# Counting edges into a dense matrix on one core: one register load for two chunks, one count of groups for all tiles, rings of four, and sums copied three windows late

## What is computed

```python
edge_index = jnp.stack([src, dst])
x = _layernorm(x + _L0_gnn_ref(x, edge_index, L0_gnn_gamma), axis=-1)
x = _layernorm(x + _L1_gnn_ref(x, L1_gnn_qW, L1_gnn_kW, L1_gnn_vW, src, dst), axis=-1)
x = _layernorm(x + _L2_gnn_ref(x, L2_gnn_weights, L2_gnn_loop_w, L2_gnn_bias, src, dst, edge_type_8), axis=-1)
x = _layernorm(x + _L3_gnn_ref(x, L3_gnn_W0, L3_gnn_b0, L3_gnn_W1, L3_gnn_b1, L3_gnn_W2, L3_gnn_b2, src, dst), axis=-1)
```

```python
def prop(h):
    return jax.ops.segment_sum(h[src] * norm, dst, num_segments=n)
```

## Time and profile before

| | |
|---|---|
| median of 3 runs | 2363.64 us |
| lowest and highest | 2362.68 and 2366.68 us |
| the profiled execution's own time | 2366.91 us |
| its span, first to last instruction | 2365.2 us |
| busy, share of the span | PE 91%, PEld 76%, DVE 77%, ACT 49%, POOL 37% |
| mean granted clock of TensorE | 0.96 of full speed |

### The profile page before, as it was taken

One profiled execution on the slowest core, in us unless ns is written; L12 is line 12 of the kernel. 1 busy time (PEld: TensorE's weight loads), 2 busy tenths in 40 slices (PEclk: granted clock), 3 DMA queues, 4 the chain that ended last, 5 costly groups with the idle time before them and its releaser, 6 DMA issues. The chain is left out here.

```text
span 2365.2 us, 63175 instructions
## 1 busy us (share of the span) xinstructions
PE 2159.4 (91%) x22505; PEld 1795.4 (76%) x22506; DVE 1832.0 (77%) x2687; ACT 1162.6 (49%) x2789; POOL 879.4 (37%) x1062
## 2 busy tenths in 40 slices
PE   2888888799999999888999978999999999999897
PEld 2777777799999999622222225999996799999787
DVE  8899988765655566578999976988886788887446
ACT  1888888432332333388999966231322432230323
POOL 3444444000000000067888832555552455555000
PEclk8999999899999999989999979999998999999899
DMA  2344444200100000242222224223224322222800
GB/s 67 153 166 165 164 166 159 106 30 30 43 30 30 29 29 15 65 108 57 57 57 59 57 97 159 84 73 88 75 60 127 139 74 77 85 75 45 343 11 22
DMA packets 94785, 205.64 MB, mean 87 GB/s; under 512 B 21718, under 2 KB 61270, under 8 KB 94450
## 3 DMA queue, kind: packets, MB, share of 16 engines
q1 hardware_dynamic: 81458, 182.46, 22.3%
q0 software_dynamic: 13120, 20.18, 4.3%
HBM read 116.99 MB, written 84.76 MB: 85 GB/s over the span
## 5 line engine op out<-in xcount | busy, mean ns | idle before, releaser
L1873 PE MATMUL l_bank<-tab,mask 128*128 128x192 f16 x7600 | 636.3, 247 | 8.3 <-PEq L1704 3.5
L1873 PEld LDWEIGHTS l_bank<-tab,mask 128*128 128x128 f16 x7600 | 629.5, 98 | 10.8 <-issue 10.2
L1459 DVE TENSOR_SCALAR mask<-code 128x1600 int32<-128x1600 int32 x304 | 546.7, 1816 | 91.6 <-PE l_bank L1873 82.7
L1849 POOL DMA_INDIRECT ggot<-table_dram,gidx x408 | 386.2, 947 | 264.7 <-PE l_bank L1873 204.0
L1356 DVE TENSOR_TENSOR pr<-ex,count_copy 128x1568 f32<-128x1568 f32 x200 | 351.0, 1786 | 24.7 <-POOL ex L1255 12.8
L1346 ACT ACTIVATE ex<-score_pair,poss 128x784 f32<-128x784 f32 x400 | 344.0, 910 | 30.0 <-PE score_pair L1294 18.6
L1255 POOL TENSOR_SCALAR ex<-ex 128x1568 f32<-128x1568 f32 x200 | 298.5, 1493 | 78.2 <-ACT ex L1346 71.1
L891 PE MATMUL sums<-onehots,ct 128*128 128x192 f16 x3125 | 266.5, 250 | 11.6 <-issue 7.3
L891 PEld LDWEIGHTS sums<-onehots,ct 128*128 128x128 f16 x3125 | 263.9, 99 | 14.1 <-issue 7.9
L891 PE MATMUL sums<-u,ct 128*128 128x192 f16 x3125 | 259.1, 246 | 0.0
L891 PEld LDWEIGHTS sums<-u,ct 128*128 128x128 f16 x3125 | 258.0, 98 | 0.0
(11 more groups left out here) (344 smaller groups left out, 2873.0 us busy)
## 6 DMA issues: line engine op xcount, KB each, us to landing
code<-code_dram SPq DMA_DIRECT2D x38, 800.0 KB
code_dram<-flat SPq DMA_DIRECT2D x100, 200.0 KB, 1.9
ct_dram<-ct SPq DMA_DIRECT2D x25, 800.0 KB, 3.5
c_dram<-flat SPq DMA_DIRECT2D x25, 800.0 KB, 3.4
ct_again<-ct_dram SPq DMA_DIRECT2D x25, 800.0 KB, 17.3
cring<-c_dram SPq DMA_DIRECT2D x200, 98.0 KB, 1.9
table_dram<-tab SPq DMA_DIRECT2D x50, 384.0 KB, 2.3
flat<-code_dram SPq DMA_DIRECT2D x19, 800.0 KB, 4.4
```

The costliest lines, as they stand in the source:

```text
L1459: e.tensor_scalar(turned.rearrange("p (s q d) -> p s q d", q=NQ, d=DQ // 2), words.rearrange("p (q s d) -> p s q d", q=NQ, d=DQ // 2), abs ...
L1849: e.indirect_dma_start(ggot[:, k, j, :], None, table_dram[:, :], bass.IndirectOffsetOnAxis(ap=gidx[:, k, j:j + 1], axis=0)).then_inc(s_ggo ...
L1873: mm = e.matmul(acc[k][:, 0:2 * D], mask[:, r % MR, s, :], tab[:, s, r, :], start=(r == 0 and s == 0), stop=(r == R - 1 and s == NT - 1))
```

## The change

The counts stage and the last step of its table change:

- The two first chunks of a window are packed into one table entry, the second one times 2048 (FIRST_BITS is 11) plus the first. GpSimd loads one register for a group and takes it apart by a mask and a shift; each chunk number is then limited to 2 NCHP, and `edges` has six more empty columns there.
- One instruction of VectorE takes the maximum of the 25 numbers of groups. Each engine loads it once, before its loop over tiles, and every window runs that many groups.
- `sel` and `col` get rings of four (SELS) instead of two; `col` moves into another buffer.
- ScalarE copies the sums of window w-3 (OUT_LAG) behind the selection of window w. The PSUM ring stays three.
- The first turn round stands after window 2 instead of 1, and its copy `row_out` one window later.

```diff
-                    e.tensor_copy(mi[:, 0:WPS], mc[:, 0:WPS]).then_inc(s_tab, 1)
+                    both_halves = mc[:, 0:WPS].rearrange("t (w h) -> t w h", h=2)
+                    e.scalar_tensor_tensor(mi[:, 0:WPT], both_halves[:, :, 1], float(1 << FIRST_BITS), both_halves[:, :, 0],
+                                           ALU.mult, ALU.add).then_inc(s_tab, 1)
...
-        turned_after = {1: 0, 3: 1, 4: 2, 5: 3}
+        turned_after = {2: 0, 3: 1, 4: 2, 5: 3}
         RECS = 4
+        SELS = 4
+        OUT_LAG = 3
...
-            def groups_of(e, t):
-                return load(e, tile_tab[0:1, bass.ds(t, 1), WPS], 1, NCHP // GRP)
+            def most_groups(e):
+                e.wait_ge(s_top, 1)
+                return load(e, top_groups[0:1, 0:1], 1, NCHP // GRP)
...
                         with e.Fori(0, groups) as g:
+                            e.reg_mov(pair, load(e, tile_tab[0:1, bass.ds(t, 1), w], 0, (1 << 2 * FIRST_BITS) - 1))
                             chunks = []
-                            for h in range(2):
-                                first = load(e, tile_tab[0:1, bass.ds(t, 1), 2 * w + h], 0, 2 * NCHP - GRP)
+                            for by, op in (((1 << FIRST_BITS) - 1, ALU.bitwise_and), (FIRST_BITS, ALU.logical_shift_right)):
+                                e.reg_alu(first, pair, by, op)
+                                e.reg_mov(first, g * GRP + e.snap(first))
+                                e.reg_alu(first, first, 2 * NCHP, ALU.min)
                                 chunks.append(nc.s_assert_within(
-                                    e.snap(g * GRP + first), 0, 2 * NCHP - GRP,
+                                    e.snap(first), 0, 2 * NCHP,
...
                 def _(e):
                     c = Chain(e, s_prep)
+                    e.tensor_reduce(top_groups[:], tile_tab[:, :, WPT], AX_X, ALU.max).then_inc(s_top, 1)
...
-                    n, past, free = three(e, "act")
+                    n = e.alloc_register("cnt_act_done")
+                    past = [e.alloc_register(f"cnt_act_past{k}") for k in range(SELS)]
...
-                        e.reg_mov(free, past)
-                        e.reg_mov(past, n)
+                        free = past[0]
+                        for k in range(SELS - 1):
+                            e.reg_mov(past[k], past[k + 1])
+                        e.reg_mov(past[SELS - 1], n)
...
                     def tile(t, first, second, last=False):
-                        groups = groups_of(e, t)
                         for w in range(WPT):
                             chosen(t, w, groups)
-                            if w >= 2:
-                                window_out(t, w - 2, first)
+                            if w >= OUT_LAG:
+                                window_out(t, w - OUT_LAG, first)
                             elif not first:
-                                window_out(t - 1, WPT - 2 + w, second)
+                                window_out(t - 1, WPT - OUT_LAG + w, second)
```

More of the change, by code:

```diff
@@ L59 @@
 NCHG = -(-NCH // GG) * GG
+FIRST_BITS = 11
 EXP_LOW = math.exp(-10.0)
@@ L390, in gnn_kernel @@
             rec_sv = wqk[:, 114:114 + RECS * 2 * PAIR].bitcast(F16).rearrange("p (k g c) -> p k g c", k=RECS, c=4)
-            sel = wqk[:, 162:162 + 2 * PAIR].bitcast(F16).rearrange("p (k c g) -> p k c g", k=2, c=2)
-            col = wqk[:, 174:174 + PAIR].bitcast(BF16).rearrange("p (k g) -> p k g", k=2)
-            assert 114 + RECS * 2 * PAIR <= 162
+            sel = wqk[:, 162:162 + SELS * PAIR].bitcast(F16).rearrange("p (k c g) -> p k c g", k=SELS, c=2)
+            col_at = 2 * PAIR * (P + WC) + 2 * NW
+            col = onehots[:, col_at:col_at + SELS * PAIR].bitcast(BF16).rearrange("p (k g) -> p k g", k=SELS)
+            assert col_at + SELS * PAIR <= NT * 2 * D
+            assert 114 + RECS * 2 * PAIR <= 162 and 162 + SELS * PAIR <= 2 * D
             s_rec = sem("cnt_rec")
@@ L428, in _, with records @@
                         e.reg_mov(r, 0)
-                    def records(t, w, groups):
+                    groups = most_groups(e)
+                    pair, first = (e.alloc_register("cnt_" + k) for k in ("pair", "first"))
+                    def records(t, w):
                         free = past[0]
@@ L436, in records @@
                         with e.Fori(0, groups) as g:
+                            e.reg_mov(pair, load(e, tile_tab[0:1, bass.ds(t, 1), w], 0, (1 << 2 * FIRST_BITS) - 1))
                             chunks = []
-                            for h in range(2):
-                                first = load(e, tile_tab[0:1, bass.ds(t, 1), 2 * w + h], 0, 2 * NCHP - GRP)
+                            for by, op in (((1 << FIRST_BITS) - 1, ALU.bitwise_and), (FIRST_BITS, ALU.logical_shift_right)):
+                                e.reg_alu(first, pair, by, op)
+                                e.reg_mov(first, g * GRP + e.snap(first))
+                                e.reg_alu(first, first, 2 * NCHP, ALU.min)
                                 chunks.append(nc.s_assert_within(
-                                    e.snap(g * GRP + first), 0, 2 * NCHP - GRP,
-                                    skip_runtime_bounds_check_because="the table's first chunk leaves room for all groups"))
+                                    e.snap(first), 0, 2 * NCHP,
+                                    skip_runtime_bounds_check_because="the minimum is the first of the empty chunks behind the table"))
                             e.wait_ge(s_col, e.snap(free) + 1)
@@ L450, in _ @@
                     with e.Fori(0, NT) as t:
-                        groups = groups_of(e, t)
                         for w in range(WPT):
-                            records(t, w, groups)
+                            records(t, w)
                 @block.vector
@@ L655, in _ @@
                     tile(NT - 1, False, False, True)
-                    window_out(NT - 1, WPT - 2, False)
-                    window_out(NT - 1, WPT - 1, False)
+                    for w in range(WPT - OUT_LAG, WPT):
+                        window_out(NT - 1, w, False)
                     for q in range(NR):
```

29 lines of the change are left out of this document (17 added, 12 removed).

## The result

| | before | changed |
|---|---|---|
| median | 2363.16 us (4 runs) | 2349.6 us (4 runs) |
| lowest to highest | 2361.87 to 2366.68 us | 2345.39 to 2352.06 us |
| the profiled execution's own time | 2366.91 us | 2352.06 us |
| first to last L474 (now L492) | 375.2 us | 360.3 us |
| ratio of the runs, 95% interval | | 0.9935 [0.9919, 0.9951] |

The kernel is 0.65% faster, 15.4 us by the ratio (times 2363.16). I had forecast 35. The sign was right and the time lies at the upper edge of the range, but the gain is less than half of the one forecast. All of it is in the counts stage: 14.9 us by the two traces.

What follows compares the result with a forecast made beforehand. GpSimd's sequencer was taken to bound the counts stage at 14.91 us a tile; at 13.5 us, 24.875 tiles make 335.8, plus 4.3 and 0.3: 340.4 against 375.2, 35 us less. Forecast 2329 us, range 2314 to 2350.

Steps and rivals of the forecast that it cites:

- What bounds the kernel now: Counts stage: GpSimd's sequencer bounds it, 13.46 us of steps plus 1.45 of stretched loads, 14.91 us a tile.
- One load for two chunks: GpSimd's window: one load and two register instructions go, arithmetic comes; 1.59 us falls to 1.41.
- my upper bound: GpSimd's window at worst: fused instructions at 0.141 us each, 0.05 more in L445's own, 1.58 us.
- the whole walk of VectorE: One tile followed at 1.64 us a window on VectorE: 13.1 us plus 0.45 of stalls, 13.5 us.
- One count of groups: GpSimd's step across a tile's end: one load with its pause goes, 0.31 us of the extra 0.74.
- The long loads: GpSimd's loads stretched behind stores: at most all 1.45 us a tile kept, though half as many can be caught.
- What is late next: After GpSimd, VectorE sets the tile: 1.64 us a window, 13.1 us; TensorE 12.4, ScalarE 12.0.
- the two stalls: VectorE waits 0.25 us at window 7 for ScalarE's selection and 0.2 at window 2 for TensorE.
- A: Rival: GpSimd stays the bound through register arithmetic or slowed copies, 14.5 us a tile, 2349 us; chance 0.12.
- D: Rival: lag of three meets ring of three if GpSimd's window stays 1.59 us; 0.6 a tile, 2379; chance 0.04.
- B: Rival: VectorE without stalls, tile 13.1 us, 10 us more gain than forecast, 2319 us; chance 0.2.
- C: Rival: ScalarE's register moves cost 0.05 us a window, tile 13.9 us, 10 us less gain, 2339; chance 0.2.

Runs made afterwards that it cites:

- e4: Changed kernel with fixed chunk numbers instead of GpSimd's table load and arithmetic (counts of the wrong edges): 2336.26 us, ratio 0.9869, stage 346.3 us.
- e7: Changed kernel with each 800 KB store issued as four, packets of 1600 bytes instead of 6400: 2339.99 us, ratio 0.9898, stage 348.9 us.
- e9: Changed kernel with the registers of past counts used in rotation instead of moved along, on GpSimd and ScalarE: 2336.81 us, ratio 0.9882.
- e8: e4 with the sums copied with a lag of two instead of three: 2330.88 us, ratio 0.9859, stage 342.0 us.
- e3: Kernel before with the order alone (rings of four, lag of three, turn rounds after windows 2 to 5), loads as before: ratio 1.0023, 5 us slower.
- e2: Kernel before with one load for two chunks alone, each tile loading its own count: ratio 0.9934, 16 us faster, stage 360.7 us.
- e12: Changed kernel with the sums copied with a lag of two instead of three, nothing else: 2348.55 us, ratio 0.9941, stage 357.6 us.
- e1: Kernel before with the one count of groups alone, loaded once by each engine: ratio 0.9983, 4 us faster, stage 372.3 us.
- e5: Kernel before with one count of groups and both chunk numbers loaded by one instruction into two registers, no arithmetic: 2344.54 us, ratio 0.9927.

## Why the prediction was wrong where it was

*What bounds the kernel now:* right. GpSimd's sequencer set the stage, and the loads held by stores were part of its beat. e4, e7 and e9 each shorten that beat in another way, and the stage follows down to the next bound.

*One load for two chunks:* **this step failed.** I priced the two fused register instructions at 0.08 us each for three operations and took 1.41 us for the window; they take 0.203 and 0.136. With them comes a move of 0.034, the `reg_mov` of `pair` in the diff, which the rows of the order leave out, so that it was four instructions for three. The arithmetic costs 0.034 + 0.032 + 0.203 + 0.136 = 0.405 us and one more pause of some 0.03, where 0.376 went. The two fused instructions at the copies, which were to be dearer at worst, became cheaper, 0.096 to 0.051 us each in the mean, and the window is 1.585 us. That my upper bound was 1.58 is luck: both of its terms were off, and they cancel. What I took from between the bounds was a guess, and the rest of the sum hung on it: with GpSimd at 1.585 us a window it stays the bound, and the whole walk of VectorE, which gave the 13.5 us a tile, does not apply.

*One count of groups:* 0.41 us at a tile's end against 0.31 forecast, 24 times, 9.9 us. This is most of what the change gained.

*The long loads:* I kept 1.45 us a tile as the worst case and expected half as many to be caught. In the changed kernel 33.4 us of 35.1 are left: hardly fewer loads are held, 87 of 201 instead of 91 of 425. From GpSimd's first copy to its last the account is 9.9 us at the tiles' ends, 1.3 in the windows and 1.8 of held time: 13.0, and the traces have 372.4 against 359.4. The other 1.9 us of the stage's 14.9 lie at its two ends, where VectorE now starts 0.9 us later behind GpSimd and ends 1.1 us closer to it. And no stretch was covered by a ring that GpSimd fills ahead, since it never got to wait for the ring.

*What is late next:* the two stalls are where the walk put them, as e4 shows, and the one at window 2 has the cause that it named, as e8 shows. Their sizes were too small: the step to window 2 is 0.35 us longer than 1.64 instead of 0.2 and the one to window 7 0.34 instead of 0.25, and with small losses in between the tile is 13.87 us instead of 13.5. So even with no register work on GpSimd at all the stage gained 28.9 us, not 35.

*Rivals:* A is what happened: 1.58 us a window and 14.5 us a tile. I gave it 0.12. Its 2349 us against 2349.6 is luck in part: 14.91 less 14.5 is 0.4 us a tile, not 0.6, so that the sum done as for the forecast gives 10 us less and 2353. A's other road, copies slowed beside VectorE, did not matter, since a pair takes 1.31 us at most and no wait follows from it. D did not come: its condition, a window of 1.59 us, holds in e3, and its waits are there, but the 5 us are held loads. B and C could not show, since GpSimd stayed the bound.

What stays open is why the held loads didn't halve with the loads in the changed kernel, when they fell by a third in e2. e3 and e12 show that the order alone, with GpSimd's own instructions left as they are, moves the held time by 7.2 us up and 3.4 us down. So what counts is where the stores fall against the loads. GpSimd, the stores and the order run in step, tile after tile, and a shorter beat can bring the loads into a store that they had missed; e1 looks the same. No run here places a store on purpose, so this is argued, not shown. Rings of four for `sel` and `col` were never tried without the other parts of the order either.

## What to carry to other kernels

An engine whose busy share is the lowest can be the bound through its sequencer: ask for the register instructions line by line and add them up to the step between two copies. Before a load is traded for arithmetic, count the arithmetic at the dearest row of its kind, or take away something else first, such as registers that are moved along where names could rotate. To tell whether the engine at a chain's start is held, look for pauses of its sequencer before its wait instructions, not at the releaser of its idle time. And test a longer lag by itself: here it helped in no run. While GpSimd was the bound it shifted only which loads were held, and once GpSimd was ahead it cost 4.3 us (e4 against e8).

## What the runs showed of the hardware

- On GpSimd a single move took 0.029 to 0.035 us, a fused register instruction 0.106 for the shifting of a ring of four, and 0.136 to 0.208 for each of the two that take a pair apart behind the mask. These two together, 0.34 us, cost more than a register load of 0.28.
- A register load from SBUF is held by stores from SBUF to DRAM: 0.28 us in the mean with none under way, 0.72 us in the mean and 0.90 at most in the changed kernel with packets of 6400 bytes, 0.45 and at most 0.58 in e7 with packets of 1600. A packet of 6400 bytes took 0.25 us in the mean, one of 1600 bytes 0.07.
- One instruction that loads two registers took 0.51 us, and 1.50 us in the mean beside packets of 6400 bytes (e5): it is two loads in time.
